# Edge masks made tile by tile, slots copied out in pairs of tiles, and a shorter path for the overflow rows

## The reference

```python
h = relu(layernorm(x))                              # per node, 64 features
e = concat([h[dst], edge_attr], axis=1)             # per edge, 64 + 64
e = relu(e @ W1.T + b1)
e = relu(e @ W2.T + b2)                             # per edge, 128
summed = segment_sum(e, src, 6250)                  # to the source node
cnt    = segment_sum(ones, src, 6250)
agg    = summed / maximum(cnt, 1)[:, None]
z = relu(concat([h, agg, u[0]], axis=1) @ Wa.T + ba)
out = x + z @ Wb.T + bb
```

## Time and profile before

| | us |
|---|---|
| times of three runs | 1935.98, 1921.0, 1929.52 |
| median | 1929.52 |
| span of the profiled execution | 1917.2 |
| GpSimd: first scatter begins | 69.1 |
| GpSimd: last scatter begins | 1853.9 |
| busy: TensorE, GpSimd, ScalarE, VectorE | 1737.8, 1528.8, 1433.6, 1289.0 |

### The profile page before, as it was taken

The page is one execution under the profiler, slowest core; times in us unless marked ns, Lnnn a source line. Parts: engine busy times, 40 slices in busy tenths (PEclk is TensorE's granted clock), DMA queues, the critical chain, the costliest instruction groups (busy, mean ns, idle before and its releaser), DMA issues.

```text
span 1917.2 us, 43265 instructions
## 1 busy us (share of the span) xinstructions
PE 1737.8 (91%) x12472; PEld 1470.5 (77%) x12472; DVE 1289.0 (67%) x4235; ACT 1433.6 (75%) x2975; POOL 1528.8 (80%) x991
## 2 busy tenths in 40 slices
PE   6898888999999999999999999999999999978837
PEld 4677666888888888888788788888888888867725
DVE  8565555667767676777776777777776676756727
ACT  4788887878888877788788787878877877862306
POOL 8488888888888888888888888888888888888850
PEclk8999999999999999999999999999999999998969
DMA  9988888999999999999999999999999999999856
GB/s 329 269 166 151 151 151 149 187 198 193 198 192 192 201 190 196 201 192 192 200 197 187 185 199 198 200 193 197 204 194 198 191 199 199 197 183 234 176 116 217
DMA packets 319400, 372.10 MB, mean 194 GB/s; under 512 B 42272, under 2 KB 203264, under 8 KB 318528
## 3 DMA queue, kind: packets, MB, share of 16 engines
q1 hardware_dynamic: 182400, 305.12, 55.6%
q0 software_dynamic: 135360, 62.15, 34.4%
q10 hardware_dynamic: 1408, 2.03, 0.3%
HBM read 203.87 MB, written 159.27 MB: 189 GB/s over the span
## 4 chain that ended last, share of the span: by engine, by line
POOL 44%; issue 19%; PE 17%; DMA 11%; DVE 5%; ACT 3%; SPq 1%; ACTq 0%; POOLq 0%; DVEq 0%
POOL sums L821 39%; DMA sums<-regA,idx 7%; POOL sums L809 5%; PE bank L1361 4%; PE bank L1350 4%; PE bank L1399 3%; PE bank L1373 3%; DVE regC L1215 2%; PE bank L1389 1%; DMA regC<-slots 1%; DMA regA<-sums 1%; DMA sums<-vscat,vidx 1%; ACT regA L931 1%; DVE regC L1182 1%; PE bank L1275 1%
## 5 line engine op out<-in xcount | busy, mean ns | idle before, releaser
L821 POOL DMA_INDIRECT sums<-regA,idx x844 | 1333.9, 1580 | 291.7 <-issue 244.4
L1350 PEld LDWEIGHTS bank<-h,regC 128*128 128x128 f32 x3072 | 389.0, 194 | 183.1 <-ACT h L943 134.0
L1350 PE MATMUL bank<-h,regC 128*128 128x130 f32 x3072 | 421.7, 281 | 63.0 <-ACT h L943 62.8
L1373 PE MATMUL bank<-regA,L 128*128 128x512 f32 x806 | 435.8, 623 | 4.6 <-DVE regA L1147 3.0
L1399 PE MATMUL bank<-w,h 128*128 128x128 f32 x3224 | 431.3, 277 | 0.0
L923 ACT ACTIVATE h<-bank,b1c 128x512 f32<-128x512 f32 x403 | 275.7, 684 | 198.0 <-PE bank L1373 193.1
L1399 PEld LDWEIGHTS bank<-w,h 128*128 128x128 f32 x3224 | 398.0, 194 | 1.1 <-ACT h L923 0.6
L1215 DVE TENSOR_SCALAR regC<-lows,regC 128x128 f32<-128x128 f32 x1176 | 257.7, 315 | 147.6 <-DMA regC<-slots 124.0
L1361 PE MATMUL bank<-regC 128*128 128x129 f32 x2352 | 298.3, 281 | 34.4 <-issue 19.0
L943 ACT ACTIVATE h<-bank 128x512 f32<-128x512 f32 x403 | 240.9, 598 | 111.1 <-PE bank L1399 107.2
L1361 PEld LDWEIGHTS bank<-regC 128*128 128x128 f32 x2352 | 277.2, 193 | 41.8 <-issue 38.1
(11 more groups left out here) (142 smaller groups left out, 1540.3 us busy)
## 6 DMA issues: line engine op xcount, KB each, us to landing
regC<-slots SPq DMA_DIRECT2D x294, 260.0 KB, 5.6
regA<-in_ea SPq DMA_DIRECT2D x202, 256.0 KB
slots<-regC SPq DMA_DIRECT2D x192, 260.0 KB
src<-rows_src SPq DMA_DIRECT2D x107, 256.0 KB
slots<-regC SPq DMA_DIRECT2D x192, 138.1 KB
sums<-regA,idx POOLq DMA_INDIRECT x844
dstR<-rows_dst SPq DMA_DIRECT2D x101, 128.0 KB
sums<-zeros SPq DMA_DIRECT2D x20, 645.0 KB, 7.0
```

Of the source, the lines that this page charges most:

```text
L821: nc.gpsimd.indirect_dma_start(out=sums[k], out_offset=bass.IndirectOffsetOnAxis(ap=idx[:, n % RING, t:t + 1], axis=0), in_=scat[:, n % 4, ...
L1350: last = T.matmul(psSlot(t)[:, k, :], place, h2[:, g % 2, t, :], start=True, stop=True)
L1373: T.matmul(psL1(s % 2), L[:, s % RING, :], R[:, s % RING, :], start=True, stop=True).then_inc(l1_done, 1)
```

## The change

1. The mask of a plain group, one tensor-tensor comparison over 512 columns with two inputs in SBUF, becomes four tensor-scalar comparisons of 128 columns, with the tile's source numbers as a scalar per partition.
2. ScalarE copies a sorted group's places out in two instructions of 520 columns instead of four of 260. It waits for both tiles of the pair, and TensorE waits for the pair's copy before tile 2.
3. The even sorted group's overflow sum is written by VectorE straight into `V`; only the odd one's goes through `vpre` and a DMA. The waits for `V` to be free move from SyncE to VectorE.
4. The key row is made by a transpose instead of a matmul with the identity.

```diff
-                if is_sorted(s - VREAD):
-                    n = BINNED_NO[s - VREAD]
-                    j, half = n // 2, n % 2
-                    sp.wait_ge(vpre_ready, n + 1)
-                    if half == 0:
-                        wait(sp, vsum_done, j - 1)
-                        wait(sp, vidx_ready, j - 1)
-                    sp.dma_start(V[half * OVER:(half + 1) * OVER, j % 2, :], vpre[:, half, :]).then_inc(v_in[n % 4], 16)
+                if closes(s - VREAD):
+                    j = BINNED_NO[s - VREAD] // 2
+                    sp.wait_ge(vpre_ready, 2 * j + 2)
+                    sp.dma_start(V[OVER:2 * OVER, j % 2, :], vpre[:, :]).then_inc(v_in[j % 2], 16)
...
-            def evac_slots(g, t):
+            def evac_slots(g, pair):
-                n = BINNED_NO[g]
-                act.wait_ge(slot_done, TPG * n + t + 1)
-                if t == 0:
+                n, t = BINNED_NO[g], 2 * pair
+                act.wait_ge(slot_done, TPG * n + t + 2)
+                if pair == 0:
                     wait(act, slot_out[n % 2], 32 * (n // 2))
                     wait(act, vpre_ready, n - 1)
-                nc.scalar.activation(slot_sb[:, n % 2, :, t, :], psSlot(t), ACT.Copy).then_inc(slot_ready, 1)
+                nc.scalar.activation(slot_sb[:, n % 2, :, t:t + 2, :].rearrange("p h t c -> p t h c"), psSlots, ACT.Copy).then_inc(slot_ready, 1)
...
-                    VE.tensor_tensor(S[:, n % 4, :, :], sB_of(g).rearrange("p (t e) -> p t e", t=TPG), srcF[:, TPG * g:TPG * (g + 1)].unsqueeze(2).broadcast_to([P, TPG, TILE]),
-                                     ALU.is_equal).then_inc(mask_ready, 1)
+                    for t in range(TPG):
+                        made = VE.tensor_scalar(S[:, n % 4, t, :], sB_of(g)[:, t * TILE:(t + 1) * TILE], srcF[:, TPG * g + t:TPG * g + t + 1], None, ALU.is_equal)
+                    made.then_inc(mask_ready, 1)
...
-                    dve.wait_ge(slot_ready, TPG * (n + 1))
-                    if n >= 2:
-                        dve.wait_ge(v_in[(n - 2) % 4], 16 * ((n - 2) // 4 + 1))
+                    dve.wait_ge(slot_ready, 2 * (n + 1))
+                    j, half = n // 2, n % 2
+                    if half == 0:
+                        wait(dve, vsum_done, j - 1)
+                        wait(dve, vidx_ready, j - 1)
+                    elif j >= 1:
+                        dve.wait_ge(v_in[(j - 1) % 2], 16 * ((j - 1) // 2 + 1))
...
-                    VE.tensor_tensor(vpre[:, n % 2, :], vhalf[:, 0, :], vhalf[:, 1, :], ALU.add).then_inc(vpre_ready, 1)
+                    VE.tensor_tensor(V[0:OVER, j % 2, :] if half == 0 else vpre[:, :], vhalf[:, 0, :], vhalf[:, 1, :], ALU.add).then_inc(vpre_ready, 1)
...
-                if t >= 2:
-                    pe.wait_ge(slot_ready, TPG * n + t - 1)
+                if t == 2:
+                    pe.wait_ge(slot_ready, 2 * n + 1)
...
-                    for n in (2 * j, 2 * j + 1):
-                        pe.wait_ge(v_in[n % 4], 16 * (n // 4 + 1))
+                    pe.wait_ge(vpre_ready, 2 * j + 1)
+                    pe.wait_ge(v_in[j % 2], 16 * (j // 2 + 1))
...
-                    T.matmul(psVrow, V[:, j % 2, C:W].broadcast_to([P, P]), ident[:, :], start=True, stop=True).then_inc(vrow_done, 1)
+                    T.transpose(psVrow, V[:, j % 2, C:W].broadcast_to([P, P]), ident[:, :]).then_inc(vrow_done, 1)
```

More of the change, by code:

```diff
@@ L314, in build @@
         earlier = sb("earlier", [P, 2, TPG], bf16)
-        vpre = sb("vpre", [OVER, 2, W], f32)
+        vpre = sb("vpre", [OVER, W], f32)
         vhalf = sb("vhalf", [OVER, 2, W], f32)
@@ L385, in psSlot @@
             return bank[:, 6 + t % 2, 0:2 * W].rearrange("p (h c) -> p h c", h=2)
+        psSlots = bank[:, 6:8, 0:2 * W].rearrange("p t (h c) -> p t h c", h=2)
         def psZ(c):
@@ L467, in build @@
         slot_out = [sem(f"slot_out{k}") for k in range(2)]
-        v_in = [sem(f"v_in{k}") for k in range(4)]
+        v_in = [sem(f"v_in{k}") for k in range(2)]
         earlier_ready = sem("earlier_ready")
@@ L604, in _ @@
                     n = BINNED_NO[s - QLAG]
-                    sp.wait_ge(slot_ready, TPG * (n + 1))
+                    sp.wait_ge(slot_ready, 2 * (n + 1))
                     sp.dma_start(slots[n, 0:HEAD, :], slot_sb[OVER:P, n % 2, 0, :, :].rearrange("p t c -> p (t c)")).then_inc(slot_out[n % 2], 16)
                     sp.dma_start(slots[n, HEAD:PLACES, :], slot_sb[:, n % 2, 1, :, :].rearrange("p t c -> p (t c)")).then_inc(slot_out[n % 2], 16)
-                if is_sorted(s - VREAD):
-                    n = BINNED_NO[s - VREAD]
-                    j, half = n // 2, n % 2
-                    sp.wait_ge(vpre_ready, n + 1)
-                    if half == 0:
-                        wait(sp, vsum_done, j - 1)
-                        wait(sp, vidx_ready, j - 1)
-                    sp.dma_start(V[half * OVER:(half + 1) * OVER, j % 2, :], vpre[:, half, :]).then_inc(v_in[n % 4], 16)
+                if closes(s - VREAD):
+                    j = BINNED_NO[s - VREAD] // 2
+                    sp.wait_ge(vpre_ready, 2 * j + 2)
+                    sp.dma_start(V[OVER:2 * OVER, j % 2, :], vpre[:, :]).then_inc(v_in[j % 2], 16)
                 for k, q in LOADS_AT.get(s, ()):
@@ L776, in scatter_all @@
                 n = BINNED_NO[g]
-                pool.wait_ge(slot_ready, TPG * (n + 1))
+                pool.wait_ge(slot_ready, 2 * (n + 1))
                 if g - 1 >= 0:
@@ L933, in _ @@
                     evac_slots(g, 0)
-                    evac_slots(g, 1)
                 g = s - 1
@@ L944, in _ @@
                 if is_sorted(s - 2):
-                    evac_slots(s - 2, 2)
-                    evac_slots(s - 2, 3)
+                    evac_slots(s - 2, 1)
                 g = s + 2
@@ L1324, in free_sums @@
                 elif is_sorted(g):
-                    pe.wait_ge(slot_ready, TPG * (BINNED_NO[g] + 1))
+                    pe.wait_ge(slot_ready, 2 * (BINNED_NO[g] + 1))
             def free_row(s):
@@ L1454, in _ @@
             pe.wait_ge(scat_ready, len(PLAIN))
-            pe.wait_ge(slot_ready, TPG * NH)
+            pe.wait_ge(slot_ready, 2 * NH)
             pe.wait_ge(vscat_ready, NV)
```

## The result

| | median, us | runs | ratio to before |
|---|---|---|---|
| before | 1925.26 | 4 | |
| changed | 1897.22 | 4 (1896.53 to 1902.48) | 0.9854 [0.9824, 0.9884] |

The change is 1.5% faster, 1897.2 us, where 0.8%, 1914 us and a range from 1901 to 1937 were forecast. Of the 17 us between the two times 4 are the baseline: with a fourth run the median of before went from 1929.5 to 1925.3. The other 12 or so are gain that the sum didn't have. The profiled execution of the changed kernel took 1902.48 us for a span of 1900.7, so a time is its span and 1.8 us. By that the profiled execution of before was one of 1919 us, under its median by 6 us, and the changed kernel's is 5 us over its own. Between the two profiles lie 16.5 us, between the medians 28.

What follows compares the result with a forecast made beforehand. GpSimd was taken as a wall of scatters: masks -15.8 us and +0.2 us for the first groups take the span from 1917.2 to 1901.6, the median from 1929.5 to 1914 us (0.8%), TensorE's +2 not counting; range 1901 to 1937.

Steps and rivals of the forecast that it cites:

- SyncE's relief: Overflow part: 96 of 192 transfers leave SyncE's queue, 0.92 us each, 89 us in all; no term in the sum.
- GpSimd as the wall: Bound: 940 scatters at 1.85 us fill 1739 of 1786 us; only scatter length or starving GpSimd moves the end.
- Is GpSimd still the wall then?: Check in the sum: TensorE's side can follow, 7 us of reserve are left, so the gain stays whole.
- The reserve of 12 us: Time by which `scat` is ready before its first scatter at the 193rd plain group: 1707.8 - 1695.9 = 12 us.
- more than the masks: Rival: sooner loads also cut landing waits and other stretching; gain 20 to 30 us, time 1905; chance 0.17.
- other 17 us of stretching: In that rival: scatter stretching not due to the masks, part of which goes as scatters land with less company.
- The masks' term: On GpSimd: 17.0 us of scatters held by masks go, 1.2 us come with the new ones; -15.8 us.
- The formula of a hold's length squared: In the series rival: a hold of length b costs scatters b²/2/1.85 per mask; 18 us for 211 old masks.
- held by the series as by one long operation: Rival: the four comparisons hold GpSimd without a break; 14 us slower, 1944, or up to 1992; chance 0.11.
- Copies and key row: On TensorE: paired copies cost +12 us, the key row's dropped pass saves 10 us; +2 us together.
- The late start: Tile 2's weight load on TensorE comes 0.06 us late behind the pair's copy, in 185 of 192 groups; +12 us.
- the pass that went: Key row by transpose has one pass instead of two, 96 x 0.11 = 10 us off TensorE's queue.

Runs made afterwards that it cites:

- overflow_alone: Kernel before with only the shorter overflow path (96 transfers for 192 on SyncE's queue), masks, copies and key row as before; 1914.3 us, ratio 0.9933.
- masks_alone: Kernel before with only the four tensor-scalar comparisons per mask; 1919.2 us, ratio 0.9970.
- masks_and_overflow: Kernel before with the four comparisons per mask and the shorter overflow path, single copies and key row by matmul kept; 1904.4 us, ratio 0.9888.
- extra_transfer: Changed kernel with 96 spare transfers put back on SyncE's queue at the places of the removed ones; 1925.6 us, ratio 0.9989.
- spare_on_scalar: Changed kernel with 96 spare transfers of the removed ones' size, issued by ScalarE's queue instead of SyncE's; 1899.7 us, ratio 0.9855.
- overflow_undone: Changed kernel with the old overflow path back (192 transfers on SyncE's queue), masks, pairs and key row as changed; 1929.3 us, ratio 1.0007.
- masks_undone: Changed kernel with the one two-input mask per plain group put back, all other parts kept; 1909.2 us, ratio 0.9920.
- two-input quarters: Changed kernel with each mask in four two-input comparisons of 128 columns in place of four tensor-scalar ones; 1901.9 us, ratio 0.9869.
- onehot_quarters: Changed kernel with VectorE's one-hot of dst (L1143) made in four instructions of 128 columns; 1907.7 us, ratio 0.9896.

## Why the prediction was wrong

**SyncE's relief: the step that failed.** The prediction priced the overflow part as "89 us in which later loads are issued sooner" and gave it no term in the sum. It is worth 10 us alone (overflow_alone), and beside the new masks 15 to 32 us: 15 from masks_alone to masks_and_overflow (1919.2 to 1904.4), 26 from extra_transfer to spare_on_scalar (1925.6 to 1899.7), 32 from overflow_undone to the changed kernel (1929.3 to 1897.2). By masks_undone the change without its masks gives 15 us and the masks 12 more; the forecast was 0 and 15.6. I never added up how full SyncE's queue was, since the page doesn't count issuing as busy. The Trainium skill says in "DMA: Bandwidth & Descriptors" (section "Issuing engines are not separate DMA queues") that starting transfers from several engines saves only the sequencer's time, which is usually small beside the transfer; here that time was the limit, as spare_on_scalar against extra_transfer shows, 0.9855 to 0.9989.

**GpSimd as the wall: right, but not alone.** "Only what shortens or stretches a scatter, or starves GpSimd, moves the end" stands. But the question at the end of the sum, "Is GpSimd still the wall then?", was answered with "TensorE's side is held back by GpSimd and can follow". masks_alone shows that with SyncE's queue as it was it couldn't: 18 us less stretching brought 5 us. In the changed kernel it could, since its loads came in time. I read the slack from ScalarE's 54.6 us of waits for `scat`, 37.6 of which lie before 700 us, and from TensorE's busy share behind 1400 us. VectorE's 219 us of load waits, the sign of the late loads, were in the same list and went unused. The reserve of 12 us was their work too, as its 10 us and 21 to 23 us in the runs above show.

**The rival "more than the masks".** Its range (a gain of 20 to 30 us) came true at 28, at a chance of 0.17, and loads that come sooner are the right beginning. The ways from there to the time are only half right. The "other 17 us of stretching" stayed: 34.4 us in all in overflow_alone. GpSimd's waits for landed scatters fell in overflow_alone (L821's own from 12.8 to 6.3 us), but in the changed kernel they are 18.1. What it lacks is that TensorE's side would else have held back the masks' gain.

**The masks' term: right in the stretching.** Forecast -15.8 us in the masks, measured 17.0 to 1.1; in time the masks are worth 12 us beside the relief and 5 without. The counts of scatters in the prediction (84, 73 and 146) come out a little lower by the trace's times (79, 70 and 142), with the same losses for the mask and the one-hot. The formula of a hold's length squared fits the old form (18 us for 17.0), is too high for two-input quarters (6 for 4.0), and would give 5 us for the tensor-scalar ones, which lost 1.1, because those let a scatter begin in their first 0.1 us. VectorE's busy time rose by 51 us, not 35, the masks' own by 55. The rival "held by the series as by one long operation" fell: 112 scatters in the series lost 1.1 us. The page "SBUF — State Buffer" of the Trainium skill (section "Who interferes with whom"), by which a mask with both inputs in SBUF would not hold descriptor writing, disagrees with this case's runs there: 17.0 us were lost to the old mask. What it does count as contended is GpSimd's reads, and a scatter's indices lie in SBUF; no run tells which of the two was held. Its other half, that a tensor-scalar operation in its two-port mode locks GpSimd out while it runs, isn't refuted: tensor-scalar operations do hold scatters here, 6.0 us at the one-hot, though whether they ran in that mode no run shows. It speaks of single instructions, so the rival of one long hold claimed more than the page does.

**Copies and key row: right for all that the runs tell.** The late start is 0.07 us for 0.06, the key row has 96 passes for 192, and in the time neither shows. That the pass that went was worth 10 us of TensorE's queue no run shows apart.

**The sum and the median.** The span came out at 1900.7 for 1901.6 forecast. That this number hit is chance: the profiled execution of before lies 6 us under its median and the changed kernel's 5 us over its own, the second profile of the changed kernel has 1892.2, and I took the difference between medians to be that between two profiles. A profile's execution should be placed among the runs before its gain is carried over; here the files of before gave only its span, and the range should have been wider below for that.

## What to carry to other kernels

Where one engine looks like a wall, add up the next limits as well, the queues that only issue transfers among them: 0.4 to 1.2 us for each issue and some 1.2 us for each register read with its address filled nine tenths of SyncE's time, and the sign was another engine's waits for transfers. Behind one limit a second of nearly the same height eats the gain: 18 us less stretching brought 5 us until SyncE's queue was relieved. Long VectorE instructions whose inputs are all in SBUF are worth cutting up beside indirect DMAs issued by GpSimd, as long as VectorE has the time; onehot_quarters shows that it can cost more than it gives.

## What the runs showed of the hardware

- A scatter issued by GpSimd that starts within a VectorE instruction can end late by that instruction's remaining time less some 0.13 us. At the two-input mask of 0.69 us this begins with starts 0.05 us behind its own and makes up to 2.08 us of 1.545; at the tensor-scalar one-hot of 0.49 us it begins 0.1 us behind and makes up to 1.80.
- The two-input comparison of 0.96 us with one input in PSUM held none of the 111 scatters that began within it (0.03 us in all, changed kernel).
- Of four 128-column instructions in a row (0.28 us each) a scatter loses 10 ns on average with one tensor input and 40 ns with two.
- In this kernel 96 transfers of 60 rows x 512 bytes cost 26 us of the time on SyncE's queue (1899.7 to 1925.6) and nothing that can be measured on ScalarE's, where each began within 10 ns of the start of the activation before it.
- A transposed float32 pass of 128 columns has the duration of a matmul's pass (273 and 275 ns), and one call has one pass for two.
